# A Mamba stack and a mixture of experts on one core: the four looping engines' loop heads placed at the first slot of a fetch block

## The chip, the cores and the metric

The kernel runs on one core of one Trainium2 chip. The metric is the device time of one execution in microseconds (us). The reader meets five engines: TensorE (PE for its matmuls, PEld for the weight loads that go with them), VectorE (DVE), ScalarE (ACT), GpSimd (POOL) and SyncE (SP, which only issues transfers here). Each engine has a sequencer that reads its own list of instructions from memory; a "q" behind an engine's name in a view (DVEq, PEldq) marks an instruction that the sequencer handles alone.

## The reference

Input x is 4 batches x 1024 tokens x 256 features. It is normalised per token, giving xn. Two branches read xn, and the output is x + s * g.

```
for i in range(8):                      # s: eight Mamba layers
    x = x + mamba_layer(x, ...)
# in one layer, per token t of 1024 and channel c of 512, 16 states n:
xz = x @ Wi.T ; xin, z = split(xz)
xin = silu(causal_conv(xin, 4 taps) + b)
delta = softplus(dt_raw @ Wdt.T + bdt)
h[c,n] = h[c,n] * exp(delta[c] * A[c,n]) + delta[c] * xin[c] * B[n]
y[c] = sum_n h[c,n] * C[n] + D[c] * xin[c]
out = (y * silu(z)) @ Wo.T
# g: silu of a top-1 mixture of 8 experts (256 -> 1024 -> 256, exact gelu), scaled by the top probability
```

The layers follow one another, and inside a layer the state h runs through the 1024 tokens in order, so the layers' part is one long chain.

## The kernel before, in words

The program has three parts, one after the other: `experts` (normalisation, routing and the mixture; fully unrolled), `mamba` (the eight layers) and `finish` (gate and final sum; fully unrolled). The change is in `mamba`.

`mamba` cuts the work into 64 units. A unit is one half (512 tokens) of one batch row in one layer, so 8 layers x 4 batches x 2 halves. In a unit the 16 states are stepped through one by one, and for each state four blocks of 128 channels: 64 scans of 128x512 in all. For a scan ACT makes the decay exp(delta*A) into a PSUM pair (L784), POOL multiplies du by the broadcast row of B (L743, eight buffers), and DVE runs the scan (L930, `scan` with its waits from L916 on). PE then turns the state so that tokens are rows (L1085, `turn_state`), ACT weighs it with C (L791, `weigh`), and PE turns it back, adding up over the states in PSUM (L1092, `turn_back`). Between these, in hand-placed positions, stand the projections (L1125, L1133, L1141, L1155, L1162), the convolution (L965, L969), softplus (L988 to L998), du (L978), the marks of overflow (L939, L941) and the gate (L1028): the tables `RING_AT`, `SILU_AT`, `CONV_AT`, `SOFT_AT`, `DU_AT` and the like (lines 79 to 97) say at which (state, block) of a unit each is issued. The parts of unit U+1 and U+2 are so laid between the scans of unit U. All order between engines goes by semaphores with absolute counts; no engine waits for all others anywhere inside `mamba`.

`units` (L596 to L604) lays the units out for one engine. Units 0 and 1 are written out ahead of the loop, units 62 and 63 behind it, and units 2 to 61 are a loop of 30 turns with two units in each. PE, DVE, ACT and POOL each have this loop, with their own counter and their own branch; SP has none, its 64 units are unrolled. Each engine reaches its loop head and its loop end when its own instructions come there, and no barrier joins them.
In the last instructions of a turn and the first of the next, DVE runs two scans (L930) across the branch, then du (L978), one step of the convolution (L969), five scans, and the gate of the unit before (L1028).

Of the kernel before, what the change touches and what calls it, by code (L numbers as in the profile page):

```python
# [40 lines left out]
ITERS = LAYERS * BATCH  # L41
# [489 lines left out]
def mamba(nc, w_in, w_x, w_dt, w_out, par, xres, ident, alive_dram, bc_dram):  # L531

    with ExitStack() as ctx:
# [62 lines left out]
        def units(eng, unit):  # L596

            unit(0, 0, 0, "first")
            unit(1, 1, 0, "mid")
            with nc.Fori(1, ITERS - 1, 1, engines=[eng.engine], hint_back_edge=True) as it:  # L600
                for h in range(HALVES):
                    unit(HALVES * it + h, h, it, "mid")
            unit(UNITS - 2, 0, ITERS - 1, "near")
            unit(UNITS - 1, 1, ITERS - 1, "last")  # L604
# [77 lines left out]
        def _(pool):  # L682
# [87 lines left out]
            halo(0, 0)  # L770
            mask_x(0, "pre1", 1, 1, 0)
            units(pool, unit)

        @block.scalar
        def _(act):
# [130 lines left out]
            exponent(0, 0, 0)  # L906
            exponent(0, 0, 1)
            units(act, unit)
            for t in range(TC):
                weigh(UNITS, 0, "end", ("S", "prev", t), UNITS - 1, STATES - 1, t)  # L910

        @block.vector
        def _(dve):
# [147 lines left out]
            for n in range(STATES):  # L1061
                for j in range(CB):
                    early(0, 1, "pre1", 1, 0, n, j)
            units(dve, unit)
            for j in range(CB):
                gate(UNITS - 1, 1, j)
# [298 lines left out]
```

## Time and profile before

| | us |
|---|---|
| median of 3 runs | 8064.28 |
| lowest and highest run | 8061.31, 8072.2 |
| the profiled execution, its own time | 8078.57 |
| its span, first to last instruction | 8076.8 |
| of it the loop, from the first hint (POOL 769.7) to the last branch (ACT 7805.8) | about 7036 |
| mean granted clock of TensorE, share of full speed | 0.971 |

The page gives the span, the busy time of every engine, the DMA queues (queue 8 and queue 14 carry instructions, queue 1 the transfers that SP issues) and the costliest groups of instructions. The timeline gives one engine's instructions in order, those of one kind merged ("x4"), with the idle time before them and who ended it in square brackets. A sequencer's own instructions, the loop's branch among them, are not in the timeline; the view of one source line shows them.

### The profile page before, as it was taken

What the parts mean: (1) busy time and instruction counts of PE and PEld (TensorE: products, weight loads), DVE (VectorE), ACT (ScalarE), POOL (GpSimd) and SP (SyncE); (2) the same over time, 40 slices, a digit from 0 to 9 for tenths busy, and PEclk for the clock granted to TensorE, in tenths of its full rate; (3) what the DMA queues carried; (4) which work ended last, traced back from release to release, by engine and by line L of the source; (5) the groups of instructions that cost most, each with busy time, mean ns of one, the idle gap of its engine ahead of it and who ended that gap; (6) DMA issues with size and microseconds to landing.
All of it is one profiled execution on the core that took longest, in us unless ns stands there. A gap on an engine that the chain in (4) does not pass through costs nothing. (4 is left out here: it accounts for less than half of the span.)

```text
span 8076.8 us, 143189 instructions
## 1 busy us (share of the span) xinstructions
PE 6817.6 (84%) x39539; PEld 4773.9 (59%) x39539; DVE 6885.2 (85%) x6710; ACT 6451.8 (80%) x10242; POOL 6100.4 (76%) x5283
## 2 busy tenths in 40 slices
PE   4978888888888888888888888888888888888887
PEld 3645655655665656556555655665565566556655
DVE  2249889988988898889889988988998898889888
ACT  1248888888888888888888888888888888888886
POOL 2137877887888788888877887887788778878875
PEclk9989999999999999999999999999999999999998
DMA  5111111111111111111111111111111111111112
GB/s 167 34 33 38 38 35 44 41 38 37 41 40 40 38 38 41 42 38 38 38 42 40 38 38 38 41 40 36 37 44 41 38 37 40 41 39 38 37 37 88
DMA packets 205422, 348.52 MB, mean 43 GB/s; under 512 B 24976, under 2 KB 63664, under 8 KB 204496
## 3 DMA queue, kind: packets, MB, share of 16 engines
q1 hardware_dynamic: 201216, 329.67, 15.2%
q0 software_dynamic: 3408, 9.33, 0.3%
q8 instruction: 364, 5.96, 0.3%
q14 instruction: 434, 3.56, 0.1%
HBM read 318.04 MB, written 20.88 MB: 42 GB/s over the span
## 5 line engine op out<-in xcount | busy, mean ns | idle before, releaser
L743 POOL TENSOR_TENSOR drive<-du,brep 128x512 f32<-128x512 f32 x4096 | 5610.7, 1396 | 856.1 <-DVE du L978 641.1
L784 ACT ACTIVATE ps_d<-delta,cur 128x512 f32<-128x512 f32 x4096 | 2827.0, 690 | 867.1 <-DVE state L930 846.3
L1085 PE MATMUL ps_r<-ident,state 128*128 128x128 f32 x16384 | 2575.0, 281 | 565.1 <-ACT prod L791 338.6
L791 ACT ACTIVATE prod<-ps_r,bcT 128x512 f32<-128x512 f32 x4096 | 2784.7, 680 | 262.5 <-PE ps_r L1085 250.8
L930 DVE TENSOR_TENSOR_SCAN state<-ps_d,carry,drive 128x512 f32<-128x512 f32 x2048 | 2518.9, 1265 | 274.9 <-ACT ps_d L784 138.1
L930 DVE TENSOR_TENSOR_SCAN state<-ps_d,drive 128x512 f32<-128x512 f32 x2048 | 2394.1, 1205 | 280.2 <-ACT ps_d L784 139.4
L1092 PE MATMUL ps_y<-ident,prod 128*128 128x128 f32 x16384 | 2508.6, 278 | 27.6 <-ACT prod L791 25.4
L1085 PEld LDWEIGHTS ps_r<-ident,state 128*128 128x128 f32 x16384 | 1867.4, 143 | 878.3 <-ACT prod L791 558.0
L1092 PEld LDWEIGHTS ps_y<-ident,prod 128*128 128x128 f32 x16384 | 1960.3, 143 | 694.5 <-issue 489.1
L1125 PE MATMUL ps_r<-xm,w_inx_sb 128*128 128x512 f32 x1024 | 534.3, 648 | 189.6 <-ACT prod L791 181.9
L969 DVE SCALAR_TENSOR_TENSOR xc<-xpad,taps,xc 128x512 f32<-128x512 f32 x768 | 657.4, 856 | 2.9
L1133 PE MATMUL ps_r<-xm,w_inz_sb 128*128 128x512 f32 x1024 | 510.0, 621 | 126.0 <-ACT prod L791 125.8
L1162 PE MATMUL ps_r<-relu,w_out_sb 128*128 128x512 f32 x1024 | 471.6, 604 | 5.6 <-ACT prod L791 3.0
L1125 PEld LDWEIGHTS ps_r<-xm,w_inx_sb 128*128 128x128 f32 x1024 | 180.2, 195 | 384.3 <-issue 198.5
L1155 PE MATMUL ps_r<-xdbl,w_dt_sb 16*128 16x512 f32 x512 | 299.9, 666 | 84.2 <-ACT soft L837 51.4
L1133 PEld LDWEIGHTS ps_r<-xm,w_inz_sb 128*128 128x128 f32 x1024 | 174.6, 190 | 312.7 <-ACT prod L791 169.1
L729 POOL COPY carry<-state 128x4 f32<-128x4 f32 x512 | 189.7, 371 | 182.1 <-DVE state L930 179.6
L1162 PEld LDWEIGHTS ps_r<-relu,w_out_sb 128*128 128x128 f32 x1024 | 185.3, 191 | 202.2 <-issue 189.0
L1103 PE MATMUL ps_y<-u,skip 128*128 128x512 f32 x512 | 283.8, 692 | 23.5 <-DVE relu L1028 23.5
L1141 PE MATMUL ps_r<-u,w_x_sb 128*48 128x512 f32 x512 | 234.9, 602 | 54.4 <-ACT u L809 54.4
L425 ACT ACTIVATE hid<-ps_t,b_sb 128x128 f32<-128x128 f32 x312 | 84.8, 382 | 227.4 <-PE ps_t L386 227.4
L353 POOL DMA_INDIRECT ys_dram<-yb,row x39 | 37.2, 955 | 294.4 <-DVE yb L445 294.4
(136 smaller groups left out, 4471.4 us busy)
## 6 DMA issues: line engine op xcount, KB each, us to landing
brep<-bc_dram SPq DMA_DIRECT2D x1024, 256.0 KB, 3.3
w_sb<-w SPq DMA_DIRECT2D x8, 1024.0 KB, 17.9
w_all<-w SPq DMA_DIRECT2D x8, 1024.0 KB, 13.0
xs_dram<-nothing SPq DMA_DIRECT2D x1, 5011.5 KB, 35.0
xb<-xs_dram SPq DMA_DIRECT2D x39, 128.5 KB, 2.0
w_all<-x SPq DMA_DIRECT2D x1, 4096.0 KB, 14.7
w_inx_sb<-w_in SPq DMA_DIRECT2D x8, 512.0 KB, 4.0
w_inz_sb<-w_in SPq DMA_DIRECT2D x8, 512.0 KB, 4.0
```

The lines of the kernel that those rows point to most:

```text
L743: nc.gpsimd.tensor_tensor(drive[:, k % DRIVE, :], du[:, j, :], brep[:, n % BREP, :], ALU.mult).then_inc(drive_set, 1)
L784: nc.scalar.activation(ps_d[:, k % 2, :], delta[h][:, j, :], ACT.Exp, scale=cur[h][:, a:a + 1]).then_inc(decay_set, 1)
L791: nc.scalar.activation(prod[:, t, :], ps_r[:, item_place(U, h, kind, item), :], ACT.Copy, scale=bcT[(h + 1) % 2 if item[1] == "prev" else ...
L930: nc.vector.tensor_tensor_scan(state[n % 2][:, j, :], ps_d[:, k % 2, :], drive[:, k % DRIVE, :], carry[:, n, j:j + 1] if h == 1 else 0.0, ...
L969: step = nc.vector.scalar_tensor_tensor(xc[:, j, :], xpad[:, j, tap:tap + T], w, xc[:, j, :], ALU.mult, ALU.add)
L1085: last = nc.tensor.transpose(out[:, j * P:(j + 1) * P], state[n % 2][:, j, t * P:(t + 1) * P], ident[:])
L1092: last = nc.tensor.matmul(ps_y[:, j, t * P:(t + 1) * P], prod[:, t, j * P:(j + 1) * P], ident[:], start=False, stop=True, is_transpose=Tru ...
L1103: last = nc.tensor.matmul(ps_y[:, j, :], skip[:, j, :], u[:, j, :], start=True, stop=True, skip_group_check=True)
L1125: last = nc.tensor.matmul(out, w_inx_sb[:, k, j * P:(j + 1) * P], xm[h][:, k, :], start=(k == 0), stop=(k == DB - 1))
L1133: last = nc.tensor.matmul(out, w_inz_sb[:, k, j * P:(j + 1) * P], xm[hf][:, k, :], start=(k == 0), stop=(k == DB - 1))
L1155: nc.tensor.matmul(out, w_dt_sb[:, j * P:(j + 1) * P], xdbl[0:RANK, :], start=True, stop=True).then_inc(ring_ready, 1)
L1162: last = nc.tensor.matmul(out, w_out_sb[:, j, k * P:(k + 1) * P], gated[:, j, :], start=(j == 0), stop=(j == CB - 1))
```

## The change

The loop gets one more argument. It asks, for the engine that lays out its units, that the loop's first instruction (the hint) be loaded at slot 0 of a fetch block, a fetch block being the 256 instruction slots that the loader counts in. The space between the code ahead of the loop and that slot is left unused and branched over once, when the loop is entered. Without the argument the head stands wherever the code ahead of it ends. Body, hint, branch, waits and order of the instructions stay as they are; all code behind the head moves by the same distance as the head.

```diff
             unit(0, 0, 0, "first")
             unit(1, 1, 0, "mid")
-            with nc.Fori(1, ITERS - 1, 1, engines=[eng.engine], hint_back_edge=True) as it:
+            with nc.Fori(1, ITERS - 1, 1, engines=[eng.engine], hint_back_edge=True,
+                         head_slot={eng.engine: 0}) as it:
                 for h in range(HALVES):
                     unit(HALVES * it + h, h, it, "mid")
             unit(UNITS - 2, 0, ITERS - 1, "near")
```

## Rows read from the trace of the kernel before

**Rows 1.** The page's first part: busy time, share of the span, instructions.

```profile
PE 6817.6 (84%) x39539; PEld 4773.9 (59%) x39539; DVE 6885.2 (85%) x6710; ACT 6451.8 (80%) x10242; POOL 6100.4 (76%) x5283
```

**Rows 2.** Waits, 1300 to 7300 us: who waited for whom, total us, times, longest.

```profile
ACT ps_d L784 <- DVE state L930: 682.1, 958, 4.9
POOL drive L743 <- DVE du L978: 519.7, 102, 7.1
```

**Rows 3.** Source line 600, whole span: ns min/median/max, first and last start us.

```profile
L600 POOLq BRANCH_PREFETCH_HINT  x30: 31/31/57, 769.7 to 7553.8; - x30
```

**Rows 4.** Source line 600, 1230 to 1262 us: one taken branch on POOL, DVE, PE.

```profile
L600 POOLq COMPARE_BRANCH  x1: 49/49/49, 1238.7 to 1238.7; - x1
L600 POOLq BRANCH_PREFETCH_HINT  x1: 31/31/31, 1238.9 to 1238.9; - x1
...
L600 DVEq COMPARE_BRANCH  x1: 74/74/74, 1250.7 to 1250.7; - x1
L600 DVEq BRANCH_PREFETCH_HINT  x1: 39/39/39, 1251.3 to 1251.3; - x1
...
L600 PEldq COMPARE_BRANCH  x1: 356/356/356, 1253.1 to 1253.1; - x1
L600 PEldq BRANCH_PREFETCH_HINT  x1: 36/36/36, 1253.5 to 1253.5; - x1
```

**Rows 5.** Timeline of DVE where the loop is entered (start us, us, instruction).

```profile
781.74 2.45 DVE L930 TENSOR_TENSOR_SCAN state<-ps_d,carry,drive 128x512 f32<-128x512 f32 x2
...
792.75 0.69 DVE L1028 TENSOR_TENSOR relu<-ps_y,zs 128x512 f32<-128x512 f32 x1 [1.15 <-PE ps_y L1092]
```

**Rows 6.** Timeline of DVE around a taken branch, 1250 to 1264 us.

```profile
1250.44 2.44 DVE L930 TENSOR_TENSOR_SCAN state<-ps_d,carry,drive 128x512 f32<-128x512 f32 x2
1252.81 1.19 DVE L978 TENSOR_TENSOR du<-delta,u 128x1024 f32<-128x1024 f32 x1
...
1261.44 0.69 DVE L1028 TENSOR_TENSOR relu<-ps_y,zs 128x512 f32<-128x512 f32 x1 [1.15 <-PE ps_y L1092]
```

**Rows 7.** DMA queues, 1236.5 to 1250 us, after POOL's branch.

```profile
q1 hardware_dynamic: 464, 0.86, 21.4%
```

**Rows 8.** DMA queues, 1251.5 to 1256 us, after the branches of DVE, PE, ACT.

```profile
q8 instruction: 1, 0.02, 1.8%
q14 instruction: 2, 0.02, 1.0%
```

**Rows 9.** DMA queues, 1253.6 to 1488.2 us: one turn by PE's loop.

```profile
q8 instruction: 11, 0.18, 0.3%
q14 instruction: 13, 0.11, 0.2%
```

**Rows 10.** Windows: busy us (count) per engine, PEclk, DMA share, GB/s.

```profile
1253.60:1488.20 234.60, 200.41 (x1187) 140.65 (x1186) 209.78 (x199) 197.95 (x309) 188.50 (x160) 0.98 0.16 40
...
7808.00:7814.80 6.80, 5.65 (x27) 5.64 (x27) 3.35 (x4) 4.59 (x8) 6.80 (x6) 0.50 0.14 41
```

**Rows 11.** Timeline of PE, where the loop is left (7805.2 us is PE's last branch).

```profile
7806.02 0.49 PE L1085 MATMUL ps_r<-ident,state 128*128 128x128 f32 x3
7809.15 0.37 PE L1085 MATMUL ps_r<-ident,state 128*128 128x128 f32 x1 [2.65 <-issue]
```

**Rows 12.** Timeline of PE ahead of a taken branch, 1245 to 1260 us.

```profile
1246.86 0.62 PE L1085 MATMUL ps_r<-ident,state 128*128 128x128 f32 x4
1248.47 1.98 PE L1133 MATMUL ps_r<-xm,w_inz_sb 128*128 128x512 f32 x4 [1.00 <-ACT prod L791]
1250.30 0.60 PE L1092 MATMUL ps_y<-ident,prod 128*128 128x128 f32 x4
1250.79 0.66 PE L1085 MATMUL ps_r<-ident,state 128*128 128x128 f32 x4
1251.28 0.60 PE L1092 MATMUL ps_y<-ident,prod 128*128 128x128 f32 x4
1253.00 0.66 PE L1085 MATMUL ps_r<-ident,state 128*128 128x128 f32 x4 [1.12 <-ACT zs L803]
```

## The prediction

> **What bounds the kernel now.** I read the page first. DVE is busy for 85% of the span, PE for 84%, ACT for 80%, POOL for 76% [rows 1]: four engines are nearly full, so one view of shares can't tell which of them sets the pace. The waits can. Over the middle of the loop ACT stands 682 us waiting for DVE's scans and POOL 520 us for DVE's du [rows 2]. The ring of scan, decay and drive is mostly paced by DVE. The reader should look for one thing from here on: at the place that the change touches, the head of the loop, does DVE, or somebody for whom DVE waits, ever lack an instruction?
>
> The loop's length: POOL's first hint stands at 769.7 and its last at 7553.8, thirty of them [rows 3], so a turn is (7553.8 - 769.7) / 29 = 233.9 us, and 29 branches back are taken. A change of 0.2% of the kernel, 16 us, is 0.56 us a turn. About 0.2% is also what a measurement of this kernel can tell from no change; its own three runs lie 0.13% apart.
>
> **What the branch back costs today.** Line 600 has the sequencers' records. DVE's branch starts at 1250.7 and the hint that heads the next turn at 1251.3; record by record this distance is 0.52 us in nearly all turns. PE: 1253.1 to 1253.5. POOL: 1238.7 to 1238.9 [rows 4]. The sequencer is away for 0.2 to 0.5 us. What reaches the engine? Here the program has its own control: the loop is first entered from above, with no branch, and the same instructions follow. From the pair of scans that lies across the head to the first gate: 792.75 - 781.74 = 11.01 us without a branch [rows 5], 1261.44 - 1250.44 = 11.00 us with one [rows 6]. And the scan pair lasts 2.44 us with du right on its end (1252.81), no idle time. So the branch back costs DVE nothing: one scan is already in the engine while the sequencer turns round. The margin is small, though: a scan is 1.2 us, of which the turn of 0.52 and the wait instructions behind the hint take most.
>
> **Where the instructions come from.** DMA queues 8 and 14 carry them. In the 4.5 us behind the branches of DVE, PE and ACT there are three packets, one for each of those engines [rows 8]; behind POOL's branch there is none in 11 us [rows 7], so POOL's loop stays where it is and is not loaded again. One turn by PE's loop takes 11 packets of 16 KB on queue 8, PE's, and 13 of 8 KB on queue 14 (0.18 MB / 11; 0.11 MB / 13) [rows 9]. 11 blocks of 256 slots fit a PE body of 2609 records (2373 of them the matmuls and weight loads of that window [rows 10], the others the sequencer's, counted one by one). The same count gives 599 records for DVE, 752 for ACT, 344 for POOL. The three bodies that are reloaded are loaded as they are run; none of these loads is waited for, or the two 11.0 us above would differ.
>
> What a load that is waited for looks like, the trace shows once. When PE leaves the loop (branch not taken, against the hint) its matmuls stop for 2.65 us with "issue" as the only reason, and go on [rows 11]; one packet of queue 8 falls in that gap. The granted clock is then 0.50, the 1.2 GHz level, for the next 6.8 us [rows 10]. That is my price of a missed block: 2.65 us, and with the slower matmuls at most about 5 us.
>
> **The change, part by part.**
>
> (1) The branch back, 29 times. The head moves from somewhere inside a block to its first slot. Body and hint stay, so the sequencer still makes one taken branch with the target asked for beforehand. Removed: nothing. Price 0, hidden by the scan that runs across the head. Bounds: at best the whole 0.52 us goes and all of it counted, 29 x 0.52 = 15 us; rows 5 and 6 say that none of it counts. At worst the load is missed on each turn, which is a rival below.
>
> (2) The distance from the head to the next block. It grows from less than a block to a full one. Today the second block is asked for right behind the branch [rows 8], and nothing stalls for it in the 11 us that follow. More room can't help where none lacks. Price 0.
>
> (3) The distance from the last block's start to the branch, in which the head's block is asked for again. With slot 0 PE's branch is at 2609 - 10 x 256 = 49 slots into its block. In front of the branch at 1253.1 I count back: matmuls and weight loads of the groups at 1251.28, 1250.79, 1250.30, 1248.47 and 1246.86 are 40, half of the one at 1253.00 is 4, five sequencer records: the 49th is at about 1246.9, 6.2 us ahead [rows 12]. A load needs about 3 us at most (2.65 of idle and the few tenths that were covered). It is in time with 3 us to spare. DVE (87 slots, at 128 a block), ACT (112) and POOL (88, nothing to load) have 30 us or more, since they need 0.3 us or more a record. Price 0.
>
> (4) Fewer loads. 599 records need 5 half blocks instead of perhaps 6, 752 need 6 instead of 7. Two packets of 8 KB a turn less, beside a queue 1 that moves 0.86 MB in 13 us [rows 7]. Price 0.
>
> (5) The entry, once. Now there is a branch over the unused slots. If the target block is the one that follows, it is there: 0.5 us of sequencer, hidden as in (1). If it must be fetched: up to 2.65 us. I take +1.
>
> (6) The exit, once. The missed block of PE comes some 200 slots later instead of some 20. It is moved, not removed: 0, bounds -5 (it falls into a wait of PE) and +5.
>
> Sum: 8078.57 + 1 = 8079.6 for an execution like the profiled one, which was itself 14.3 us above the median. On the median: 8064.28 + 1 = 8065.3 us.
>
> **A rule weighed.** DVE, PE and ACT leave 0.4 to 0.5 us at the branch, POOL 0.2 [rows 4]. The Trainium skill (Runtime: NRT & Kernel Launch, Instruction fetch mechanics) says that a taken branch to a target outside the two blocks held forces a fetch before execution goes on, and that otherwise fetching runs in sequence and is mostly hidden. By the first half each of the 29 branches would stall, before and after alike, and the change would be worth nothing; the trace disagrees with it on this hinted branch, as no turn shows a gap like the one of rows 11 at the head.
>
> **Rivals.**
> (a) The head's block comes late on PE (slower). PE is asked for its block only 49 slots ahead of the branch. If its sequencer ran those slots far ahead of the array, the load would be missed on every turn: 29 x 2.65 = 77 us, 8141 us, and up to 29 x 5 = 145 us if the clock falls each time. It decides once the 49 slots are passed in under 3 us. Against it: PE waits 1.00 and 1.12 us inside these slots [rows 12], and the sequencer stands with it. The same mechanism on DVE would need its 87 slots in under 3 us. Chance 5%; with smaller stalls at blocks' edges, 8%.
> (b) The turn at the branch shrinks and it does count (faster): 29 x 0.52 = 15 us, 8050 us. Against it rows 5 and 6. Little of it would pass 0.2%. Chance 7%.
> (c) The slot isn't what the chip sees: the loader's own instructions shift it, the head lands elsewhere. Then again nothing stalls today, and 8064 us. This can't be told from my forecast by time; it would show in the packets. Inside the forecast's chance.
>
> There is also noise that any shift in time re-deals: TensorE's granted clock is 0.98 over a turn [rows 10], so it sits at half speed for some us in it, and where those fall moves with the start of the loop. That can move the sum by some us either way.
>
> **How the numbers follow.** Forecast, no change that can be told: 85%, at 8065.3. Its range: -5 for the exit, -6 for the run to run spread, and the reach of (b) to 8050, give a low end of 8046; +2.7, +5 and the spread of +8 above the median, with a few us for small stalls, give 8084. Rival (a) at 8141 is left out. Faster by over 0.2%: 7%. Within: 85%. Slower: 8%.
>
> **What would show it.** Right: DVE's scan pair across the head followed by du without idle time, 11.0 us from pair to gate; branch to hint still 0.5 us; turns of 234 us; queue 8 with 11 packets a turn as before, queue 14 with 11 where 13 stand in rows 9. Wrong: "issue" gaps of about 2.65 us on PE next to the branch in every turn, or a clock that falls there; a longer branch to hint; POOL loading its loop again. What would make me wrong altogether is a turn shorter by over 0.56 us with unchanged waits in the rows, which would mean that block edges cost something that this trace doesn't show as idle time.

## The result and the profile after

| | before | after |
|---|---|---|
| median of 4 runs each, us | 8062.8 | 8180.53 |
| lowest and highest run | 8059.32, 8072.2 | 8142.65, 8182.36 |
| ratio, with its 95% interval | | 1.0136 [1.0109, 1.0163] |
| mean granted clock of the profiled execution | 0.971 | 0.962 |

The change costs 1.36% by the ratio (118 us between the two medians), where no change was forecast. The profiled execution of after is the fastest of its four, 38 us below their median, and that of before lies 16 us above its own. So the two traces show only a part of the loss: the span of after is 64 us longer than that of before.

The page of after, its span and the lines that answer to [rows 1] and to the queues of [rows 9], here over the whole span:

```profile
span 8140.9 us, 143193 instructions
...
PE 6869.4 (84%) x39539; PEld 4832.3 (59%) x39539; DVE 6882.3 (85%) x6710; ACT 6464.0 (79%) x10242; POOL 6098.2 (75%) x5283
...
q8 instruction: 364, 5.96, 0.3%
q14 instruction: 380, 3.11, 0.1%
```

DVE has the same work as before (6882 us against 6885 in [rows 1]); PE is busy 52 us longer with the same 39539 matmuls, so some of them ran slower. Queue 14 moves 380 packets where before had 434; queue 8, PE's, has the same 364. So the head did move, as the change says.

Source line 600 (L600) over the whole span of after: duration in ns as minimum, median and maximum, then the first and the last start:

```profile
L600 POOLq COMPARE_BRANCH  x31: 38/49/70, 763.8 to 7861.9; - x31
L600 DVEq COMPARE_BRANCH  x31: 57/68/92, 776.1 to 7874.0; - x31
L600 PEldq COMPARE_BRANCH  x31: 87/3381/3865, 778.6 to 7876.5; - x31
L600 ACTq COMPARE_BRANCH  x31: 38/49/73, 779.2 to 7877.0; - x31
L600 POOLq BRANCH_PREFETCH_HINT  x30: 31/31/57, 766.5 to 7625.1; - x30
```

The same view of before, PE's branch:

```profile
L600 PEldq COMPARE_BRANCH  x30: 88/357/407, 1019.1 to 7805.2; - x30
```

Here is the loss in one line. There are 31 branches instead of 30, since the entry has one now. Those of POOL, DVE and ACT last as long as ever. PE's lasts 3.38 us in the median where it lasted 0.36. The 31 of them last 85.6 us together, the 30 of before 10.5: 75.1 us more. The loop itself, from where PE enters it (in before its first hint, in after the branch over the unused slots) to its last branch, went from 7020.7 to 7098.0 us, 77.2 more. The part ahead of it was 5.9 and the part behind it 7.2 us shorter, which makes the 64 us of the spans.

One turn of after, line 600 from 1705 to 1728 us, answers to [rows 4]:

```profile
L600 DVEq COMPARE_BRANCH  x1: 68/68/68, 1721.0 to 1721.0; - x1
L600 DVEq BRANCH_PREFETCH_HINT  x1: 39/39/39, 1721.6 to 1721.6; - x1
...
L600 PEldq COMPARE_BRANCH  x1: 3524/3524/3524, 1723.4 to 1723.4; - x1
...
L600 PEldq BRANCH_PREFETCH_HINT  x1: 40/40/40, 1727.0 to 1727.0; - x1
```

DVE turns in 0.6 us. PE's sequencer starts its branch at 1723.4 and executes nothing until 1727.0. What its array does in the meantime stands in PE's timeline of the same place (start, duration, instruction, and in brackets the idle time ahead of it and who ended it):

```profile
1723.29 0.66 PE L1086 MATMUL ps_r<-ident,state 128*128 128x128 f32 x4 [1.12 <-ACT zs L804]
1727.19 1.11 PE L1093 MATMUL ps_y<-ident,prod 128*128 128x128 f32 x4 [3.25 <-issue]
1728.09 1.06 PE L1086 MATMUL ps_r<-ident,state 128*128 128x128 f32 x4
```

"3.25 <-issue": nothing that the trace shows held PE back, no semaphore and no tile; it had no instruction. This is the stop that [rows 11] show once at the exit, 2.65 us long, and it is now at the head of nearly every turn. Behind it four matmuls take 1.11 us instead of 0.60 to 0.66. The windows of after give their clock (stretch, its length, then busy time of PE, PEld, DVE, ACT and POOL, PE's granted clock, DMA share and GB/s), for a whole turn, for 3 us behind the stop and for 11 us ahead of it:

```profile
1487.90:1727.00 239.10, 204.68 (x1186) 144.40 (x1186) 209.51 (x199) 198.58 (x308) 189.15 (x161) 0.96 0.15 39
1727.00:1730.00 3.00, 2.81 (x13) 2.82 (x14) 1.31 (x2) 0.71 (x2) 3.00 (x4) 0.50 0.40 88
1712.00:1723.00 11.00, 9.06 (x52) 6.23 (x52) 11.00 (x10) 8.63 (x15) 2.96 (x2) 1.00 0.08 17
```

2.4 GHz ahead of the stop, 1.2 GHz behind it. Over all turns PE now sits at the lower level for 16.2 us a turn where it was 10.4; in the first 20 us behind the head for 5.1 us where it was 1.2.

How it reaches DVE, which sets the pace, is in the timelines of ACT and DVE of after. ACT has its weighing (L792) wait for PE's turned state:

```profile
1729.29 0.69 ACT L792 ACTIVATE prod<-ps_r,bcT 128x512 f32<-128x512 f32 x1 [2.48 <-PE ps_r L1086]
```

The decays for the next scans (L785) stand behind that weighing on ACT, and so DVE lacks them:

```profile
1720.72 2.45 DVE L931 TENSOR_TENSOR_SCAN state<-ps_d,carry,drive 128x512 f32<-128x512 f32 x2
1723.09 1.19 DVE L979 TENSOR_TENSOR du<-delta,u 128x1024 f32<-128x1024 f32 x1
...
1730.59 1.22 DVE L931 TENSOR_TENSOR_SCAN state<-ps_d,drive 128x512 f32<-128x512 f32 x1 [2.28 <-ACT ps_d L785]
...
1734.54 0.69 DVE L1029 TENSOR_TENSOR relu<-ps_y,zs 128x512 f32<-128x512 f32 x1 [0.92 <-PE ps_y L1093]
```

From the scan pair to the gate it is 13.82 us; it was 11.00 in [rows 6]. So 2.82 of PE's 3.25 us arrive at DVE. Summed up, in the waits of after from 1300 to 7300 us (who waited for whom: total us, times, longest):

```profile
DVE state L931 <- ACT ps_d L785: 258.7, 184, 2.6
...
DVE state L931 <- PE ps_r L1086: 205.8, 169, 3.2
...
PE ps_y L1093 <- issue: 68.0, 25, 3.6
```

and before:

```profile
DVE state L930 <- ACT ps_d L784: 214.5, 156, 2.5
...
DVE state L930 <- PE ps_r L1085: 169.0, 126, 3.3
```

The row with "issue" holds 25 stops, one for each turn in the window, of 2.7 us on average (why not 3.25 each time stands below); before has no such row. DVE's two waits have grown by 44.2 + 36.8 = 81 us in the same 25 turns.

Last, when the block of the head is asked for. DMA queues (packets, MB, share of 16 engines) of after, from 1705 to 1724.2 us, and then from 1724.2 to 1727.1:

```profile
q1 hardware_dynamic: 288, 0.52, 11.9%
q14 instruction: 1, 0.01, 0.1%
...
q8 instruction: 1, 0.02, 2.6%
q14 instruction: 1, 0.01, 1.1%
```

PE enters its last block at about 1717.2, 49 slots ahead of the branch. No packet of queue 8 follows until the branch has started. Before, at the turn of 1955.3, from 1936 to 1941 us:

```profile
q8 instruction: 1, 0.02, 1.8%
```

and none from 1941 up to the branch: the packet came some 14.5 us ahead of it.

Not every turn of after is like this one. In 22 of the 29 no packet of queue 8 comes between the entry of the last block and the branch, and the branch lasts 3.1 to 3.9 us. In the other seven one does come, 1.2 to 1.4 us ahead of the branch, when PE is at slot 38; the branch then lasts only 1.0 to 1.2 us. The turn of 2201.3 is one of them. Its branch, PE's next matmuls, and the queue from 2199.5 to 2201.2:

```profile
L600 PEldq COMPARE_BRANCH  x1: 1021/1021/1021, 2201.3 to 2201.3; - x1
...
2202.56 0.65 PE L1093 MATMUL ps_y<-ident,prod 128*128 128x128 f32 x4 [0.74 <-issue]
...
q8 instruction: 1, 0.02, 3.2%
```

So in after too the block is sometimes asked for ahead of the branch, but too late to hide the whole load; PE stops for 0.74 us, and its next matmuls keep their speed (0.65 us for four, at a granted clock of 1.00).

### The profile page after: what moved, and what is told of

It reads as the page before. It is cut to its first block and busy times, and to the rows that moved or that the text cites. A ratio compares the mean times of both kernels' runs of the same rounds, so it can differ in the third digit from the quotient of the medians.

```text
span 8140.9 us, 143193 instructions
## 1 busy us (share of the span) xinstructions
PE 6869.4 (84%) x39539; PEld 4832.3 (59%) x39539; DVE 6882.3 (85%) x6710; ACT 6464.0 (79%) x10242; POOL 6098.2 (75%) x5283
## 5 line engine op out<-in xcount | busy, mean ns | idle before, releaser
L785 ACT ACTIVATE ps_d<-delta,cur 128x512 f32<-128x512 f32 x4096 | 2828.8, 691 | 846.6 <-DVE state L931 825.8
L792 ACT ACTIVATE prod<-ps_r,bcT 128x512 f32<-128x512 f32 x4096 | 2792.7, 682 | 330.5 <-PE ps_r L1086 317.4
L1093 PE MATMUL ps_y<-ident,prod 128*128 128x128 f32 x16384 | 2538.7, 280 | 95.8 <-issue 78.7
L1093 PEld LDWEIGHTS ps_y<-ident,prod 128*128 128x128 f32 x16384 | 1987.6, 145 | 762.2 <-issue 578.4
L1086 PEld LDWEIGHTS ps_r<-ident,state 128*128 128x128 f32 x16384 | 1893.9, 144 | 831.7 <-ACT prod L792 510.9
```

The costliest lines, as they stand in the source:

```text
L785: nc.scalar.activation(ps_d[:, k % 2, :], delta[h][:, j, :], ACT.Exp, scale=cur[h][:, a:a + 1]).then_inc(decay_set, 1)
L792: nc.scalar.activation(prod[:, t, :], ps_r[:, item_place(U, h, kind, item), :], ACT.Copy, scale=bcT[(h + 1) % 2 if item[1] == "prev" else ...
L1086: last = nc.tensor.transpose(out[:, j * P:(j + 1) * P], state[n % 2][:, j, t * P:(t + 1) * P], ident[:])
L1093: last = nc.tensor.matmul(ps_y[:, j, t * P:(t + 1) * P], prod[:, t, j * P:(j + 1) * P], ident[:], start=False, stop=True, is_transpose=Tru ...
```

## The experiments

Eleven kernels. Each is the kernel before, with `head_slot` set for some engines alone, to 0 or to another slot; one has no `head_slot` and lacks PE's hint. The edit is the same everywhere but for the first line; an engine that `heads` does not name keeps the head where it was:

```diff
-            with nc.Fori(1, ITERS - 1, 1, engines=[eng.engine], hint_back_edge=True) as it:
+            heads = {"PE": 0}
+            heads = {eng.engine: heads[eng.engine.name]} if eng.engine.name in heads else None
+            with nc.Fori(1, ITERS - 1, 1, engines=[eng.engine], hint_back_edge=True,
+                         head_slot=heads) as it:
```

The loop's records carry line 602 in these. Where the head is moved decides where the branch falls: PE's body has 2609 records, so with the head at slot h the branch is at slot (h + 2608) mod 256. Of the kernel before it follows from the exit's stop (below) that its head stood at about slot 190 and its branch at about 238. Medians of the kernel before were 8063.33, 8084.13 and 8060.87 us in the three groups of runs, so only ratios are compared.

| kernel | PE's branch at slot | turns in which PE's block is late, of 29 | ratio to before, 95% |
|---|---|---|---|
| after: all four engines 0 | 48 | 29, 7 of them in part (branch 1.0 to 1.2 us) | 1.0136 [1.0109, 1.0163] |
| PE 0 | 48 | 29, 4 of them in part (1.2 to 1.5 us) | 1.0132 [1.0115, 1.0149] |
| the other three 0 | as before | 0 | 1.0000 [0.9990, 1.0009] |
| PE 223 | 15 | 29, 1 of them in part (1.1 us) | 1.0150 [1.0133, 1.0167] |
| PE 16 | 64 | 21 | 1.0092 [1.0068, 1.0115] |
| PE 64 | 112 | 11, all in part (1.1 to 1.6 us) | 1.0009 [0.9999, 1.0019] |
| PE 104 | 152 | 0 | 1.0004 [0.9990, 1.0018] |
| PE 186 | 234 | 0 | 0.9993 [0.9984, 1.0003] |
| PE 186, the other three 0 | 234 | 0 | 1.0003 [0.9993, 1.0013] |
| before without PE's hint | as before | 29 | 1.0150 [1.0133, 1.0167] |
| DVE 46 | as before | 0 | 0.9998 [0.9987, 1.0009] |
| ACT 20 | as before | 0 | 1.0019 [1.0009, 1.0028] |

**Which engine.** PE alone at slot 0, and the other three alone.

```diff
+            heads = {"PE": 0}
```

> Only TensorE's loop head is put at slot 0; the other three stay where they are. Theory A (TensorE asks for the head's block too late, as its branch stands in the 49th slot of the last block): all of the loss comes back, median 8140 to 8185 us, TensorE's COMPARE_BRANCH about 3.5 us long in most turns. Theory B (the loss comes from the heads of the other engines or from the four together): 8055 to 8075 us.

```diff
+            heads = {"DVE": 0, "Activation": 0, "Pool": 0}
```

> Only VectorE, ScalarE and GpSimd have slot 0; TensorE's head stays. Theory A: no loss, 8055 to 8075 us, TensorE's COMPARE_BRANCH 0.36 us. Theory B: 8140 us or more. In both queue 14 has some 54 packets less than before.

Medians 8168.98 and 8062.87 us. PE alone carries the whole loss; the other three together cost nothing and gain nothing, though queue 14 has 380 packets with them as it has in after. PE's branch with PE at slot 0, over the whole span:

```profile
L602 PEldq COMPARE_BRANCH  x31: 87/3452/3950, 779.9 to 7890.0; - x31
```

**Is it the slot or the argument.** PE at slot 186, close to where it was, but laid there by the same argument, with the same branch over unused slots at the entry; and PE at slot 64.

```diff
+            heads = {"PE": 186}
```

> TensorE's head is placed, but at slot 186, where I work out that it stood before (the missed block after the loop's end came 22 slots behind the branch). Theory A: the placing itself costs nothing, 8055 to 8075 us. Rival C (the padding or the branch over it costs, whatever the slot): 8100 us or more. If 186 is indeed the slot of before, the stop of 2.65 us with reason issue behind the loop's end is again 22 slots behind the last branch.

```profile
L602 PEldq COMPARE_BRANCH  x31: 88/357/382, 781.6 to 7787.3; - x31
...
7791.26 0.44 PE L1095 MATMUL ps_y<-ident,prod 128*128 128x128 f32 x2 [2.32 <-issue]
```

(The second line is of PE's timeline of that kernel, where the loop is left.) Median 8059.69: neither the argument nor the entry costs anything. The exit's stop stands 26 slots behind the branch here and 22 in before, which is how the slot of before was worked out.

```diff
+            heads = {"PE": 64}
```

> TensorE's head at slot 64: its branch has 112 slots of the last block in front of it in place of 49. Theory A1 (the block is asked for within some 100 slots or 9 us after the last block is entered, as the lags of before show): mostly in time, 8060 to 8080 us. Theory A2 (any place but the old one is late): near 8180 us.

```profile
L602 PEldq COMPARE_BRANCH  x31: 88/362/1567, 781.3 to 7809.6; - x31
```

Median 8074.88. The maximum, not the median, is what to read here: 11 of the turns have a branch of 1.08 to 1.57 us, the others one of 0.35 to 0.37; that makes 11.7 us in all, 0.15%, which the ratio of 1.0009 [0.9999, 1.0019] allows. Set beside the DMA queue, the 11 are those in which the packet of queue 8 came 1.0 to 1.4 us ahead of the branch, when PE had come to slot 101 of its last block; in the other 18 it came 11 to 12 us ahead. So the time of asking is not tied to the entry of a block, and it differs from turn to turn with the code unchanged.

**How much room the branch needs.** Three kernels were placed for this: PE's branch at slot 15 (less room than in after), 64 (a little more) and 152.

```diff
+            heads = {"PE": 223}
```

> TensorE's head at slot 223, far from a block's first slot, but its branch falls into the 16th slot of a new block. Theory A (what counts is how many slots of the last block stand in front of the branch): late on every turn, COMPARE_BRANCH 3 to 4 us in all 29, 8165 to 8190 us. Rival D (what counts is that the head is the first slot of a block): 8055 to 8075 us.

```profile
L602 PEldq COMPARE_BRANCH  x31: 87/3603/3868, 784.6 to 7927.4; - x31
```

Median 8195.43, a little above the expected 8190, beside a before of 8084 in this group. All 29 are late (one in part), with the longest branch in the median of all kernels that have the hint. So rival D is out: a head away from a block's first slot loses as much as one on it. One more block edge falls into the body (12 instead of 11 blocks touched), and queue 8 moves 392 packets, 28 more.

```diff
+            heads = {"PE": 16}
```

> TensorE's head at slot 16, 64 slots in front of the branch. Theory A: late in most turns, but with more of them only partly late than at slot 0: 8100 to 8170 us, between the 8169 us of slot 0 and the 8075 us of slot 64. If the loss jumps from one level to the other with no middle, it is a threshold and not a race of times.

```profile
L602 PEldq COMPARE_BRANCH  x31: 88/3135/3747, 785.8 to 7891.2; - x31
```

Median 8156.75. In 21 turns the branch lasts 3.1 to 3.7 us and in 8 it is in time (0.44 to 0.47 us), with nothing between. The time fits the expectation, the turns that would be only partly late don't occur. Queues of this kernel in the 8 us ahead of a branch in time (1252.3, which lasts 0.45 us), and ahead of a late one (1484.9, 3.12 us):

```profile
q1 hardware_dynamic: 272, 0.52, 22.9%
q8 instruction: 1, 0.02, 0.8%
q14 instruction: 1, 0.01, 0.3%
...
q14 instruction: 1, 0.01, 0.4%
```

In the 8 turns in time the block is asked for when PE is at slots 0 to 19, 5.6 to 7.0 us ahead of the branch. In the other 21 the packet comes only behind the branch's start, 0.7 to 1.2 us.

```diff
+            heads = {"PE": 104}
```

> TensorE's head at slot 104, 152 slots of the last block in front of the branch. The loads of this queue start when TensorE executes slot -10 to 115 of a block, in all kernels so far. Theory A: always in time, COMPARE_BRANCH 0.36 us in every turn, 8055 to 8072 us. If it is late in some turns, the load needs more than the 3 us that I allow it.

```profile
L602 PEldq COMPARE_BRANCH  x31: 88/443/468, 779.7 to 7784.2; - x31
```

Median 8080.68, ratio 1.0004; the expected 8055 to 8072 was counted from a before of 8063, and in this group before stands at 8084. None late, though PE's branch lasts 0.44 us and not 0.36; the packets come at slots 88 to 108, 5.7 to 7.0 us ahead. Of the slots tried, 152 is the smallest with which the block was in time in every turn. (The range of slots in the expectation is a little narrow: PE 64 has packets at slot -12.)

**What the hint is worth.** Before, with the head where it was, but no hint on PE.

```diff
+            heads = {}
...
+            with nc.Fori(1, ITERS - 1, 1, engines=[eng.engine], hint_back_edge=(eng.engine.name != "PE"),
```

> TensorE's loop has no branch hint and its old place; the other three keep theirs. Theory A: without a hint the head's block is never asked for ahead of the branch, so each of the 29 branches waits for a whole load: COMPARE_BRANCH 3.4 to 4 us, 8165 to 8200 us, the same as slots 0 and 223. Then slot 0 takes from the hint all that it gives. If this is much slower than slot 0, the hint still gives something at slot 0; if it is 8055 to 8085 us, the hint is not what hides the load.

```profile
L602 PEldq COMPARE_BRANCH  x30: 83/3476/3886, 1016.6 to 7913.4; - x30
```

Median 8184.82. Without the hint, at the best slot, PE loses as much as with the hint at slot 0 (ratio 1.0150 against 1.0136, the intervals overlap). At slot 0 the hint is thus worth nothing that the time of these kernels can tell. The traces show a little: without the hint all 29 branches last 3.3 to 3.9 us, while after has its seven of 1.0 to 1.2. Queue 8 has 392 packets again: about one more a turn than before, as if the block that follows in sequence were loaded in vain; which block it is the trace doesn't say.

**Do the others have the same edge.** DVE's branch in slot 4 of its last half block, and ACT's in slot 3.

```diff
+            heads = {"DVE": 46}
```

> Only VectorE's head is placed, at slot 46, so that its branch falls into the 5th slot of a half block of 128. VectorE's queue loads 8 KB. Theory A holds for every engine: the head's half block is asked for too late, VectorE's COMPARE_BRANCH 2 to 3.5 us in place of 0.07 us, about 1.2 us of it hidden by the scan in the engine, so 29 x 1 to 2.3 us = 30 to 65 us, 8090 to 8130 us. If the trouble is TensorE's alone: 8055 to 8075 us.

One turn of this kernel on line 602, and DVE's timeline:

```profile
L602 DVEq COMPARE_BRANCH  x1: 68/68/68, 1477.8 to 1477.8; - x1
L602 DVEq BRANCH_PREFETCH_HINT  x1: 39/39/39, 1480.1 to 1480.1; - x1
```

```profile
1477.46 2.44 DVE L933 TENSOR_TENSOR_SCAN state<-ps_d,carry,drive 128x512 f32<-128x512 f32 x2
1479.83 1.19 DVE L981 TENSOR_TENSOR du<-delta,u 128x1024 f32<-128x1024 f32 x1
...
1488.46 0.69 DVE L1031 TENSOR_TENSOR relu<-ps_y,zs 128x512 f32<-128x512 f32 x1 [1.15 <-PE ps_y L1095]
```

Median 8082.39, no loss: my expectation of some 8090 to 8130 missed. The block is late in each turn (2.25 us from branch to hint, where it was 0.52), but pair to gate is still 11.00 us. The reader can see why: du starts at 1479.83, ahead of the hint at 1480.1. It was handed to DVE before the branch, with the two scans. Three instructions, from 1477.46 to 1481.02, lay over the branch; 3.2 us of them were left when it started. The wait of 1.15 us for PE ahead of the gate is the same as in [rows 6], so it took up nothing of the delay, although the next expectation gives it as the reason.

```diff
+            heads = {"Activation": 20}
```

> Only ScalarE's head is placed, at slot 20, so that its branch falls into the 4th slot of a half block: ScalarE's distance from branch to hint grows from 0.41 to about 2.2 us, as VectorE's did at slot 46. VectorE's cost nothing, because it waits 1.15 us for TensorE right behind the head. ScalarE waits about 1.1 us for VectorE behind the head and makes what TensorE needs next. Theory E (a late load costs what is left of it after the wait that follows on the same engine): 0 to 0.7 us a turn, 8060 to 8085 us. If every late load went through to the sum: 29 x 1.8 = 52 us, 8110 us or more.

```profile
L602 ACTq COMPARE_BRANCH  x1: 49/49/49, 1483.8 to 1483.8; - x1
...
L602 ACTq BRANCH_PREFETCH_HINT  x1: 31/31/31, 1485.8 to 1485.8; - x1
```

```profile
1486.02 0.69 ACT L787 ACTIVATE ps_d<-delta,cur 128x512 f32<-128x512 f32 x1 [1.24 <-DVE state L933]
```

Median 8075.14, ratio 1.0019. From the branch to the hint it is 1.81 us in the median, where it was 0.41. ACT's next decay starts with 1.24 us of idle time ahead of it where before had 1.11, so nearly all is hidden by a wait that was there anyway. The 0.13 us would make 4 us over 29 turns, and the ratio 15; where the rest goes the profiled execution doesn't show.

**Can both be had.** PE at slot 186, the other three at 0.

```diff
+            heads = {"PE": 186, "DVE": 0, "Activation": 0, "Pool": 0}
```

> The change with one number put right: VectorE, ScalarE and GpSimd at slot 0 as in the change, TensorE at slot 186. Theory A: the whole loss goes, 8050 to 8080 us, equal to the kernel before within 0.2%. If something of the loss stays, the four heads act together in a way that single placings did not show.

Median 8065.74, ratio 1.0003 [0.9993, 1.0013]. Queue 14 has 380 packets as in after, PE's branch its 357 ns. The 54 packets saved are worth nothing that can be measured. No kernel run here beats the one before.

## Why the prediction was wrong

**The step that failed is (3)**, the distance from the last block's start to the branch. Its count was right: 49 slots, 6.2 us. What it took for granted was that the head's block is asked for when the last block is entered. With that, 6.2 us against a load of 3 left "3 us to spare". The runs show other moments. In before PE's packet comes around the start of its last block in 7 turns of 29 (slots -7 to 2), and only at slots 76 to 90 in the other 22. In PE 64 it is 18 turns at slots -12 to -8 and 11 at 100, in PE 16 eight turns at 0 to 20, in PE 104 all at 88 to 108, in PE 186 three turns at 49 to 53 and most at 70 to 82. In after, with the branch at slot 48, it is 7 turns at slot 38, 1.3 us ahead, and in the other 22 no packet comes before the branch has started, which then waits for the whole load. The trace of before held a warning. I counted packets per turn, but never looked where in the block they stand; that asks at slots 76 to 90 exist, far behind slot 48, was there to be read. One more window of the DMA view, from the entry of the last block to the branch, would have been a reason to give rival (a) more weight.

**The size of a missed block.** 2.65 us, from [rows 11], with up to 5 us where the clock falls. Measured: PE's branch lasts 3.38 us in the median, 3.0 more than before, and 3.1 to 4.0 over all kernels where the branch itself had to ask, so a whole load is a little more than the 3 us that (3) allowed; with the matmuls at 1.2 GHz behind it, the kernels with 29 late turns lose 106 to 124 us in the median, 3.6 to 4.3 us a turn. So the bounds held, and the truth is inside them: the stop itself is 3.25 us in the turn shown, not 2.65, and the slower matmuls add the rest.

**Rival (a)** is what happened, in that the head's block comes late on PE, and 8180.53 lies between its 8141 and its upper end (145 us more than before, 8209). I gave it 5 to 8%. Its deciding point, "once the 49 slots are passed in under 3 us", was wrong for the same reason: PE did take 6 us over them. The argument against it, that the sequencer stands with the array's waits, agrees with those 6 us and doesn't help.

**(1) and (5), the cover.** Price 0 on DVE, ACT and POOL was right. Its working was wrong in that "one scan" covers DVE and "the margin is small": du is handed over ahead of the branch too, and 3 us are covered, as DVE 46 shows. On PE, for which the step gave no cover of its own, there is none: its matmuls of the new turn come at once when the sequencer returns, and little is queued across the branch. At the entry DVE, ACT and POOL took 2.7 to 3.0 us from branch to hint where I had 0.5, since their block wasn't there; PE took 0.4. DVE's scan pair and du ran across it without a gap. +1 was fair.

**(2) and (4)** were right: POOL, with nothing to load, and 54 packets fewer (434 to 380; I had two a turn, 58), at no price.

**(6), the exit.** In after PE does not stop at the exit; in PE 186 it does, as in before. The part behind the loop varies from 264 to 273 us over all kernels, more than the 2.65 us in question. What the exit is worth can't be told.

**The rule weighed.** I set the Trainium skill (Runtime: NRT & Kernel Launch, Instruction fetch mechanics), by which a taken branch to a target outside the two blocks held forces a fetch before execution goes on, against the hinted branch, and found the trace against it. The runs draw the line between the two. Without the hint the trace agrees with the rule on PE: a branch of 3.3 to 3.9 us in each turn, 3.48 in the median. With the hint the stall is avoided where the branch leaves room for the ask (0.36 us in before), and is there again where it does not (3.38 us in after).

**The range.** 8046 to 8084 left (a) out, as the text said. The time of 8180.5 is not near its edge.

## What stays open

What decides in a turn between the early and the late ask. With the same code it was early in 7 of 29 turns of before, in 18 of PE 64, in 8 of PE 16, and never in PE 104, where it came at slots 88 to 108 each time. It was not tried to set it by delaying the entry of a block. There is one lead, which no run tests: in the trace of after 188 of the 279 packets of queue 8 between 1000 and 7000 us start 0.9 to 1.2 us behind a record that PE's sequencer handles itself (a register operation, a semaphore or a branch); with all packets shifted by 0.7 to 3 us, to either side, it is only 27 to 62.

That 38 us lie between the profiled execution of after and its median isn't explained either. Its seven branches of 1.0 to 1.2 us are 2.4 us shorter in the mean than the other 22, which makes 17 us, and the slower executions may have fewer such turns. That is an estimate: they have no trace.

## What to carry to other kernels

A hint on a loop's branch helps only if its block is asked for before the branch comes, and on PE that was as late as 108 slots into the block here: place the head so that the last block holds about 150 slots ahead of the branch or more (152 were enough in each turn, 112 were not in 11 of 29, 64 and fewer lost most or all). These counts are of one loop, whose last 49 slots take 6 us with two waits in them; in another loop the same slots may pass in less or more time. Slot 0 is no safe choice by itself; what counted here is head slot plus body length, modulo 256. Look at PE first, since little was queued across its branch, while DVE, with 3 us of work handed over, hid a missed block entirely.

## What the runs showed of the hardware

- **The ask for the next block isn't tied to the entry of a block.** On PE the packet stood at slots -7 to 2 or 76 to 90 in one and the same program (before), and anywhere from -12 to 108 over all kernels. In the turns with a late block it is 2.3 to 2.9 us from the packet's start to the end of the branch. Where the packet came only behind the branch's start, the branch lasted 3.1 to 4.0 us.
- **The price of a missed block differs by engine**: branch to hint became 2.25 us on DVE (0.52), 1.81 on ACT (0.41), 3.5 to 3.7 on PE (0.4). Of PE's stop nearly all reached the time (2.82 of 3.25 us in the turn shown), of DVE's nothing, of ACT's some 15 us in 29 turns by the ratio.
- **A stop of 3.25 us on PE has a tail**: the granted clock went from 1.00 to 0.50 behind it, and four matmuls from 0.60 to 1.11 us. Behind a stop of 0.74 us four matmuls still took 0.65.
